# Softmax row sums over four added steps in place of two, and two weight loads moved behind the router's next tiles

## The reference, cut to what matters

```python
q, k, v = proj(wq, bq), proj(wk, bk), proj(wv, bv)           # (B, 16, 1024, 32)
probs = softmax(einsum('bhqd,bhkd->bhqk', q, k) / sqrt(32))
ctx = einsum('bhqk,bhkd->bhqd', probs, v)
x = layernorm(x + ctx @ wo.T + bo)
scores = x @ gate_w.T                                        # router: 8 experts, the 2 best
routed = sum of the 2 chosen experts: (silu(x @ w_gate.T) * (x @ w_up.T)) @ w_down.T
shared = silu(x @ sh_gate.T) * (x @ sh_up.T) @ sh_down.T
x = layernorm(x + routed + sigmoid(x @ se_gate_w.T) * shared)
```

## Time and profile before

| what | value |
|---|---|
| median of 3 runs | 2083.41 us (2080.54 to 2083.98) |
| the profiled execution, its own time | 2082.21 us |
| its span, first to last instruction | 2080.5 us |
| PE busy | 2013.2 us, 97% |
| DVE, ACT, POOL busy | 1277.8, 879.3, 867.7 us |
| row sums (L748) on PE | 1024 matmuls, 133.9 us |
| POOL's folds (L623) | 129 + 129 + 118 adds of about 1.3 us |
| attention, router, experts end at about | 1283, 1330, 2080 us |

### The profile page before, as it was taken

One profiled execution on the slowest core, in us unless ns is written; L12 is line 12 of the kernel. 1 busy time (PEld: TensorE's weight loads), 2 busy tenths in 40 slices (PEclk: granted clock), 3 DMA queues, 4 the chain that ended last, 5 costly groups with the idle time before them and its releaser, 6 DMA issues.

```text
span 2080.5 us, 30213 instructions
## 1 busy us (share of the span) xinstructions
PE 2013.2 (97%) x9764; PEld 1222.7 (59%) x9765; DVE 1277.8 (61%) x2281; ACT 879.3 (42%) x1563; POOL 867.7 (42%) x829
## 2 busy tenths in 40 slices
PE   7999999999999999999999988999999999999997
PEld 5655555655556655556655435688444444446886
DVE  5877776677776677775677856573222222225875
ACT  2266654466664466664366674311111111112332
POOL 3255654455654455654455557200111111114651
PEclk9999999999999999999999999999999999999999
DMA  7312434312334322434321325822222222225762
GB/s 232 72 41 68 97 78 102 127 46 64 98 77 103 127 53 56 98 79 102 126 51 38 73 73 204 315 78 71 92 90 91 91 85 86 91 76 168 227 177 72
DMA packets 95922, 213.00 MB, mean 102 GB/s; under 512 B 24304, under 2 KB 24816, under 8 KB 92592
## 3 DMA queue, kind: packets, MB, share of 16 engines
q1 hardware_dynamic: 84992, 175.96, 28.7%
q0 software_dynamic: 10800, 35.40, 6.3%
HBM read 118.51 MB, written 41.93 MB: 77 GB/s over the span
## 4 chain that ended last, share of the span: by engine, by line
PE 84%; SPq 4%; DMA 3%; DVE 3%; issue 2%; POOL 2%; ACT 1%; another core or an unknown queue 1%; ACTq 0%; POOLq 0%; DVEq 0%
PE ps_gu L1684 12%; PE ps_s L724 11%; PE ps_side L702 11%; PE ps_ctx L735 10%; PE ps_side L676 8%; PE ps_gu L1622 8%; PE ps_d L1707 6%; PE ps_sum L748 5%; PE ps_d L1622 4%; SPq L359 3%; DMA inv_rows<-inv_few 2%; PE ps_t L1674 1%; PE pr_s L1254 1%; PE ps_hts L1697 1%; PE ps_side L724 1%
## 5 line engine op out<-in xcount | busy, mean ns | idle before, releaser
L999 DVE TENSOR_REDUCE max_half<-ps_side 128x1 f32<-128x512 f32 x1024 | 658.6, 682 | 202.4 <-PE ps_side L702 199.3
L702 PE MATMUL ps_side<-kq_stack 96*128 96x512 f32 x1024 | 408.9, 404 | 4.9 <-DVE max_half L999 2.3
L724 PE MATMUL ps_s<-kq_stack 97*128 97x512 f32 x937 | 392.4, 420 | 7.8 <-ACT probs_first L888 4.8
L724 PEld LDWEIGHTS ps_s<-kq_stack 97*128 97x128 f32 x937 | 177.5, 190 | 165.4 <-issue 85.5
L1578 POOL DMA_INDIRECT x_g<-x,who_all x71 | 67.3, 948 | 471.3 <-PE ps_t L1674 355.5
L1684 PE MATMUL ps_gu<-gu_sb,xT_e 128*128 x568 | 258.6, 598 | 0.8 <-issue 0.6
L888 ACT ACTIVATE probs_first<-ps_s 128x512 f32<-128x512 f32 x326 | 187.5, 600 | 106.6 <-PE ps_s L724 90.8
L702 PEld LDWEIGHTS ps_side<-kq_stack 96*128 96x128 f32 x1024 | 195.1, 191 | 57.3 <-DVE max_half L999 26.3
L888 ACT ACTIVATE probs_mid<-ps_s 128x512 f32<-128x512 f32 x308 | 177.5, 599 | 111.7 <-PE ps_s L724 97.1
L623 POOL TENSOR_TENSOR acc<-probs_first,probs_mid 128x512 f32<-128x512 f32 x129 | 163.8, 1297 | 132.2 <-ACT probs_mid L888 132.2
L888 ACT ACTIVATE probs_last<-ps_s 128x512 f32<-128x512 f32 x303 | 175.5, 599 | 98.6 <-PE ps_s L724 82.3
(11 more groups left out here) (238 smaller groups left out, 3303.2 us busy)
## 6 DMA issues: line engine op xcount, KB each, us to landing
kq_stack<-kq SPq DMA_DIRECT2D x192, 256.0 KB, 5.1
y_slots<-y_t SPq DMA_DIRECT2D x71, 256.0 KB, 2.3
x_r<-x SPq DMA_DIRECT2D x32, 256.0 KB, 3.8
x_t<-x SPq DMA_DIRECT2D x32, 256.0 KB
gu_sb<-wgu SPq DMA_DIRECT2D x8, 1024.0 KB, 15.2
out<-gu_sb SPq DMA_DIRECT2D x32, 256.0 KB, 2.6
res<-inv_rows SPq DMA_DIRECT2D x124, 64.0 KB, 2.0
stage<-wkqT SPq DMA_DIRECT2D x28, 256.0 KB, 3.1
```

The source lines that it names most:

```text
L702: nc.tensor.matmul(bank, q_stack[par][0:3 * HD, h, t * P:(t + 1) * P], k_stack[par][0:3 * HD, h, half * HALF:(half + 1) * HALF], start=Tru ...
L724: nc.tensor.matmul(out, k_stack[par][0:3 * HD + 1, h, kt * P:(kt + 1) * P], q_stack[par][0:3 * HD + 1, h, half * HALF:(half + 1) * HALF], ...
L999: nc.vector.reduce_max(max_half[:, u // 2, u % 2:u % 2 + 1], bank, AX.X).then_inc(side_free, 1)
```

## The change

`SUM = 4` sets how many steps are added up ahead of a row sum; `FOLD = 2` still sets the block of `weighted`. In a quad, step 1 writes `acc = probs(0) + probs(1)`, and steps 2 and 3 add theirs to `acc` in place. So three adds of each head run in a quad in place of two, and one `row_sums` in place of two. All waits on `folded` and `folded_dve` count anew. SP's load of `wv_lo` waits for the adds up to step 62 of the batch in place of the row sums up to step 61. The loads of the two shared weights move behind tiles 15 and 19.

```diff
+SUM = 4
-        SUMS = BSTEPS // FOLD
+        SUMS = BSTEPS // SUM
+        ADDS = SUMS * (SUM - 1)
...
+        def adds_before(loc):
+            return loc // SUM * (SUM - 1) + max(loc % SUM - 1, 0)
+        def taken_in(loc):
+            return loc if loc % SUM else loc + 1
...
                 if not last and g == G - 1:
                     sp.wait_ge(pv_done, (b + 1) * BSTEPS - FOLD)
-                    sp.wait_ge(sum_done, (b + 1) * SUMS - 1)
+                    sp.wait_ge(folded, added_pool(b, BSTEPS - 1))
+                    sp.wait_ge(folded_dve, added_dve(b, BSTEPS - 1))
...
-                for k in range(1, 3):
-                    load_shared(k)
                 for t in range(12, TT):
...
                     load_r(t)
+                    if t in (15, 19):
+                        load_shared(1 if t == 15 else 2)
...
             def fold(b, loc):
-                i = loc // FOLD
+                i = loc // SUM
                 for h in range(pool_heads(b, loc)):
                     pool.wait_ge(probs_ready, b * HEADS_B + HG * loc + h + 1)
-                    if i and h == 0:
+                    if i and loc % SUM == 1 and h == 0:
                         pool.wait_ge(sum_done, b * SUMS + i)
+                    if loc % SUM > 1:
+                        pool.wait_ge(folded, added_pool(b, loc - 1) + h + 1)
...
-                    nc.gpsimd.tensor_tensor(acc[:, h, :], probs(loc - 1, h), probs(loc, h),
-                                            ALU.add).then_inc(folded, 1)
+                    nc.gpsimd.tensor_tensor(acc[:, h, :], probs(loc - 1, h) if loc % SUM == 1 else acc[:, h, :],
+                                            probs(loc, h), ALU.add).then_inc(folded, 1)
             def batch(b, last):
...
+                    if loc % SUM:
+                        fold(b, loc)
                     if loc % FOLD:
-                        fold(b, loc)
...
             def row_sums(b, loc):
-                pe.wait_ge(folded, added_pool(b, loc // FOLD + 1))
-                pe.wait_ge(folded_dve, added_dve(b, loc // FOLD + 1))
+                pe.wait_ge(folded, added_pool(b, loc + 1))
+                pe.wait_ge(folded_dve, added_dve(b, loc + 1))
...
-                            row_sums(b, loc)
+                            if loc % SUM == SUM - 1:
+                                row_sums(b, loc)
...
-                        if slot == 1 and loc % FOLD:
+                        if slot == 1 and loc % SUM:
                             fold(b, loc)
```

More of the change, by code:

```diff
@@ L280, in pool_heads, with added_pool, added_dve @@
         def pool_heads(b, loc):
[L283 to L290, removed]
+            return HG // 2 if b == B - 1 and loc >= EVEN_FROM else HG - FOLD_DVE
+        def adds_before(loc):
+            return loc // SUM * (SUM - 1) + max(loc % SUM - 1, 0)
+        def added_pool(b, loc):
+            return sum(pool_heads(b, i) for i in range(loc) if i % SUM) + b * ADDS * (HG - FOLD_DVE)
+        def added_dve(b, loc):
+            return HG * (b * ADDS + adds_before(loc)) - added_pool(b, loc)
+        def taken_in(loc):
+            return loc if loc % SUM else loc + 1
         def base_of(m):
@@ L613, in fold @@
             def fold(b, loc):
-                i = loc // FOLD
+                i = loc // SUM
                 for h in range(pool_heads(b, loc)):
                     pool.wait_ge(probs_ready, b * HEADS_B + HG * loc + h + 1)
-                    if i and h == 0:
+                    if i and loc % SUM == 1 and h == 0:
                         pool.wait_ge(sum_done, b * SUMS + i)
-                    if i == 0 and h == 0:
+                    if loc % SUM > 1:
+                        pool.wait_ge(folded, added_pool(b, loc - 1) + h + 1)
+                    if loc == 1 and h == 0:
                         pool.wait_ge(tail_free, b * TAIL + KT)
                         pool.wait_ge(const_set, WO_MADE)
-                    nc.gpsimd.tensor_tensor(acc[:, h, :], probs(loc - 1, h), probs(loc, h),
-                                            ALU.add).then_inc(folded, 1)
+                    nc.gpsimd.tensor_tensor(acc[:, h, :], probs(loc - 1, h) if loc % SUM == 1 else acc[:, h, :],
+                                            probs(loc, h), ALU.add).then_inc(folded, 1)
             def batch(b, last):
@@ L742, in row_sums @@
                 kt = loc % KT
-                pe.wait_ge(folded, added_pool(b, loc // FOLD + 1))
-                pe.wait_ge(folded_dve, added_dve(b, loc // FOLD + 1))
-                if kt == FOLD - 1 and loc >= KT:
+                pe.wait_ge(folded, added_pool(b, loc + 1))
+                pe.wait_ge(folded_dve, added_dve(b, loc + 1))
+                if kt == SUM - 1 and loc >= KT:
                     pe.wait_ge(sum_taken, b * G * NHALF + loc // KT)
@@ L748, in row_sums @@
                     done = nc.tensor.matmul(ps_sum[h * HD:(h + 1) * HD, :], ones[:], acc[:, h, :],
-                                            start=kt == FOLD - 1, stop=kt == KT - 1)
+                                            start=kt == SUM - 1, stop=kt == KT - 1)
                 done.then_inc(sum_done, 1)
@@ L875, in exps @@
                     act.wait_ge(pv_done, b * BSTEPS + loc - PROBS + 1)
-                    if h < pool_heads(b, loc - PROBS):
-                        act.wait_ge(folded, added_pool(b, (loc - PROBS) // FOLD) + h + 1)
+                    taken = taken_in(loc - PROBS)
+                    if h < pool_heads(b, taken):
+                        act.wait_ge(folded, added_pool(b, taken) + h + 1)
                     else:
-                        act.wait_ge(folded_dve, added_dve(b, (loc - PROBS) // FOLD) + h - pool_heads(b, loc - PROBS) + 1)
+                        act.wait_ge(folded_dve, added_dve(b, taken) + h - pool_heads(b, taken) + 1)
                 elif loc == 0:
@@ L1024, in fold @@
             def fold(b, loc):
-                i, first = loc // FOLD, pool_heads(b, loc)
+                i, first = loc // SUM, pool_heads(b, loc)
                 for h in range(first, HG):
                     dve.wait_ge(probs_ready, b * HEADS_B + HG * loc + h + 1)
-                    if i and h == first:
+                    if i and loc % SUM == 1 and h == first:
                         dve.wait_ge(sum_done, b * SUMS + i)
-                    if i == 0 and h == first:
+                    if loc % SUM > 1:
+                        dve.wait_ge(folded_dve, added_dve(b, loc - 1) + h - pool_heads(b, loc - 1) + 1)
+                    if loc == 1 and h == first:
                         dve.wait_ge(tail_free, b * TAIL + KT)
                         dve.wait_ge(const_set, WO_MADE)
-                    nc.vector.tensor_tensor(acc[:, h, :], probs(loc - 1, h), probs(loc, h),
-                                            ALU.add).then_inc(folded_dve, 1)
+                    nc.vector.tensor_tensor(acc[:, h, :], probs(loc - 1, h) if loc % SUM == 1 else acc[:, h, :],
+                                            probs(loc, h), ALU.add).then_inc(folded_dve, 1)
             def batch(b, last):
```

6 lines of the change are left out of this document (3 added, 3 removed).

## The result

The changed kernel takes 2209.5 us (median of 4, 2201.7 to 2212.1) against 2083.1: ratio 1.060, 95% interval 1.058 to 1.063. The forecast was 2133 with a range of 2100 to 2168; the sign was right, the size not. In the profiled execution the span grew by 129.7 us, from 2080.5 to 2210.2. The row sums are 512 matmuls, as they should be, and the profile after shows the stalls that were foreseen, larger than foreseen, and losses in two places where a gain had been forecast: the quads called clean and the last batch.

What follows compares the result with a forecast made beforehand. PE, busy nearly throughout, was taken to bound the kernel. Terms of -21.6 + 31 + 15 + 14.4 - 5 - 5.5 + 6 + 16.5 = +51 us on 2082.2 gave 2133 us, range 2100 to 2168.

Steps and rivals of the forecast that it cites:

- x quads: Quads with x_low in groups 1 and 2: two folds behind POOL's other work make PE wait, +14.4 us over three batches.
- How POOL and DVE slow each other: In stalled quads, DVE adds beside POOL's folds lengthen POOL's adds during a quarter of a fold: +6 us, at most 35.
- Clean quads: 30 quads with nothing between POOL's folds: each gains 0.86 us less a 0.14 wait for DVE's second add, -21.6 us.
- Split quads: Two folds behind POOL's weight split make PE stand some 3.0 us in 10 groups: +31 us.
- Clock: After 10 of 16 new PE stalls the granted clock falls, costing 1.65 us each: +16.5 us, at most 54.
- Ends of three batches: `wv_lo` and all behind it on SP's queue come later: +5.0 us each, +15 us; PE's own 3.1 us lie beside.
- Rest of the last batch: Group 3 of the last batch: pairs without row sums save 1.25 us in four quads, -5 us.
- Router: Moving the shared weights' loads removes PE's idle 3.85 us and slow turns after it: -5.5 us.
- The rival of contention throughout: POOL's adds take 1.49 us and DVE's 1.30 everywhere: 41 us beyond the forecast, 2174 us; chance 10%.

Runs made afterwards that it cites:

- e11: The changed kernel with DVE's in-place adds replaced by one-operand reductions of the same 512 columns: 2135.1 us.
- e3: The changed kernel with DVE's in-place adds of steps 2 and 3 cut to one column, POOL's left whole: 2142.1 us.
- e4: The changed kernel with the in-place adds of both POOL and DVE cut to one column: 2030.6 us.
- e2: The changed kernel with POOL's in-place adds of steps 2 and 3 cut to one column, DVE's left whole: 2043.5 us.
- e6: The changed kernel with POOL's weight split moved from behind step 13 to behind step 15, PE's first two products each waiting for their half: 2141.2 us.
- e5: The changed kernel with matmuls by zero weights put where PE stood waiting for POOL: 2173.2 us.
- e8: The changed kernel with SP's load of `wv_lo` waiting for the adds up to step 61 in place of step 62: 2198.1 us.
- e1: The kernel before with only the two shared weights' loads moved behind the router's tiles 15 and 19: 2079.1 us against 2083.9, ratio 0.998.
- the best kernel: The changed kernel with pairs kept in x quads and last batch's groups 2, 3; later split, earlier `wv_lo` load and DVE step-2 add: 2056.3 us, ratio 0.988.

## Why the prediction missed

The direction was right and so were the places of the stalls behind the split and the x quads, but two terms with a gain were losses, and the sum was some 77 us short (2209.5 against 2133). Point by point:

- *How POOL and DVE slow each other (+6, bound 35).* This is the step that failed. e11 takes the mutual waiting of the in-place adds out and falls by 74 us, where the term had 6, and its attention (+60.0, the first five rows) is then close to the prediction's terms without this one (-21.6 + 31 + 14.4 + 15 - 5 + 16.5 = +50.3). I had priced it as a share, a quarter of the time of two adds beside each other. It is a turn: whoever comes second waits (DVE's add of 0.68 us takes 1.67, POOL's of 1.26 takes 1.80). I should have seen it in the earlier trace rows: DVE's add took 0.98 us there and ended 0.55 after POOL's fold (606.40 + 3.79 = 610.19), while the same add takes 0.68 alone. I also gave it to stalled quads only. By the table (changed less e11) the split and x quads and the turns lost 20.3, 16.8 and 5.2 us by it, and the clean quads and the last batch, where I had none, 16.7 and 14.3. These sums hold the clock that the longer stalls set off: the mean granted clock from 100 to 1250 us is 0.95 after the change and 0.97 in e11, some 23 us (an estimate: 0.02 x 1150). The two parts weren't measured apart. What the prediction cited of the Trainium skill (GPSIMD Engine Reference, section 8) says no more than that the two engines are in contention. The Trainium skill, SBUF — State Buffer, section "Who interferes with whom", is plainer: the shared pair of ports is an exclusive lock, a DVE instruction with two SBUF inputs contends with a GpSimd instruction that reads SBUF, and one with a single input, outside its 2-port modes, does not. e3 (0.75 to 1.02 us for one column) and e11 (0.67) agree.
- *Clean quads (-21.6).* +2.6; -24.7 in e4, so the row sums do give 0.8 each. DVE's adds alone take 11 of it back (e2), waiting for POOL the rest. DVE's second add had 0.14 us; in step 7, whose slot 0 has two `pre` units, the wait is 1.09 us behind the add of 1.67, and 0.15 or less in three of four such waits of e2, where POOL's adds are short.
- *Split quads (+31).* Right in mechanism: e6 removes them by POOL's order, with a finer wait of PE for the split. The stall was 3.99 for 3.0, 3.21 without the mutual waiting; with the clock 58 us.
- *Clock (+16.5, bound 54).* Some 36 (e5), so this term was too small as well. I had let six of sixteen stalls hide theirs, and counted 1.65 us each. Up to 1200 us PE ran at the lower level right behind every stall ahead of row sums of 1.97 us or more (it had fallen already before one of 3.03), and behind none of 1.34 or less; later, one of 2.42 at 1317 us was not followed by it.
- *x quads (+14.4).* +39, of which 17 go with e11. The other 8 beyond the forecast I put down to the clock behind stalls of 2 to 3.2 us; that is not shown.
- *Ends of three batches (+15).* +15.0, as told: SP's load is on the chain in two of the three turns, and with the load early (e8) PE's own stall, laid beside it as 3.1 each, leaves 9.3. What e8 wins is the difference, 1.9 a turn; its theory had forgotten the stall beside. That the sizes fit so well is partly luck, since PE's part holds the clock and the mutual waiting too. The count itself gives 5.1 (14.6 + 0.1 - 9.6), not 5.0.
- *Rest of the last batch (-5).* +18.2, the wrong sign. With two heads on each engine every add has another beside it (3.39 and 3.47 us for two). Alone, the saving is -9.2 (e4).
- *Router (-5.5).* -4.8 by the medians, -5.7 in the profiled execution (e1).

The rival of contention throughout, at 10%, had the mechanism in the right places but priced it at 41 us beyond the forecast; one part that it left out is the clock that longer stalls bring.

## What to carry to other kernels

Before an add is moved between VectorE and GpSimd or multiplied there, count how often two of them meet, and price each meeting as a wait for what is left of the other's running instruction (here up to 1.2 us on an add of 0.68, and 0.5 on one of 1.29); put DVE's add where DVE has nothing urgent behind it, and POOL's other work behind the folds that PE waits for. A stall of TensorE of 2 us and more is to be priced with the slower clock that nearly always followed it here, and filling it with zero matmuls shows how much of a loss that is. Take such a saving only where the engines have time: the best kernel has it in 44 of 64 quads.

## What was not expected of the hardware

- A one-column add on DVE stood through three whole adds of POOL in e3. DVE, then the first of them:

```profile
534.23 3.85 DVE L1054 TENSOR_TENSOR acc<-acc,probs_first 128x1 f32<-128x1 f32 x1
```
```profile
534.33 1.28 POOL L637 TENSOR_TENSOR acc<-acc,probs_first 128x512 f32<-128x512 f32 x1
```

  It ends 0.02 us after the last of the three. The longest took 5.0 us, while in the changed kernel no whole add took over 1.85. Why the short add gets its turn so late stays open.
- A row sum of one head costs PE as much as one of four (0.95 and 0.97 us).
- Filling stalls with work that computes nothing made the kernel 36 us faster.
